# Moving the token-shift mixes and the convolution's SiLU products from VectorE to GpSimd in a Mamba block between two FFNs, with the steps placed anew

## What is computed

```python
def ffn(x, W_r, W_k, W_v, mu_r, mu_k):              # x has been normalised per token
    x_prev = shift x by one token, zeros first
    xr = mu_r * x + (1.0 - mu_r) * x_prev            # the token-shift mixes
    xk = mu_k * x + (1.0 - mu_k) * x_prev
    r = sigmoid(xr @ W_r.T)
    return r * (square(relu(xk @ W_k.T)) @ W_v.T)

def mamba(x, ...):
    xn = layernorm(x) * ln_w + ln_b
    xs, z = split(xn @ W_in.T)                       # 1024 channels each
    xc = silu(b_conv + causal convolution of xs with 4 taps)
    dt_low, B, C = split(xc @ W_xproj.T)             # 32, 16, 16
    delta = softplus(dt_low @ W_dt.T + b_dt)
    h = exp(delta * A) * h + delta * B * xc          # 1024 channels x 16 states, token by token
    y = (h * C).sum(states) + D_skip * xc
    return (y * silu(z)) @ W_out.T + x

x = x + 0.5 * ffn(layernorm(x), ...)
x = x + mamba(x, ...)
x = x + 0.5 * ffn(layernorm(x), ...)
```

## Time and profile before

| | us |
|---|---|
| median of 3 runs | 4891.49 |
| lowest and highest | 4890.23, 4892.57 |
| span of the profiled execution | 4888.0 |
| DVE busy | 4488.3 (92%) |
| PE busy | 4296.9 (88%) |
| POOL busy | 3196.4 (65%) |
| ACT busy | 2900.1 (59%) |

### The profile page before, as it was taken

One profiled execution on the slowest core, in us unless ns is written; L12 is line 12 of the kernel. 1 busy time (PEld: TensorE's weight loads), 2 busy tenths in 40 slices (PEclk: granted clock), 3 DMA queues, 4 the chain that ended last, 5 costly groups with the idle time before them and its releaser, 6 DMA issues.

```text
span 4888.0 us, 58099 instructions
## 1 busy us (share of the span) xinstructions
PE 4296.9 (88%) x16896; PEld 2382.9 (49%) x16896; DVE 4488.3 (92%) x3650; ACT 2900.1 (59%) x6355; POOL 3196.4 (65%) x3328
## 2 busy tenths in 40 slices
PE   6777989898999989989898899989999898999787
PEld 2444545454554545545454454545545454554443
DVE  2799999999999999999999999999999999999992
ACT  2555656666666566656666665666656666665452
POOL 1666767576676767767576676767667576776770
PEclk9888999999999999999999999999999999999798
DMA  2445555454554555555555554555555565655451
GB/s 82 141 135 180 172 171 185 163 183 162 189 169 151 189 168 186 172 173 185 158 174 163 186 172 152 190 179 176 172 185 173 155 180 156 190 170 153 167 164 62
DMA packets 423053, 810.71 MB, mean 166 GB/s; under 512 B 41264, under 2 KB 41264, under 8 KB 418640
## 3 DMA queue, kind: packets, MB, share of 16 engines
q1 hardware_dynamic: 422736, 807.00, 52.1%
HBM read 772.25 MB, written 34.60 MB: 165 GB/s over the span
## 4 chain that ended last, share of the span: by engine, by line
DVE 38%; PE 29%; issue 16%; ACT 7%; POOL 6%; DMA 3%; DVEq 0%; SPq 0%; POOLq 0%; ACTq 0%
DVE decay L1091 19%; DVE g L1099 10%; PE y_acc L567 6%; PE mm L494 5%; PE mm L483 5%; POOL dbx L1298 4%; PE mm L472 4%; DVE xc L1037 3%; DMA c_all<-bc_scratch 2%; PE mm L531 2%; PE mm L509 2%; PE mm L519 2%; DVE xc L1043 1%; ACT decay L889 1%; POOL xout L1287 1%
## 5 line engine op out<-in xcount | busy, mean ns | idle before, releaser
L1298 POOL TENSOR_TENSOR dbx<-u,b_all 128x1024 f32<-128x1024 f32 x1024 | 2414.2, 2358 | 902.6 <-DVE g L1099 901.7
L1091 DVE TENSOR_TENSOR_SCAN decay<-decay,state,dbx 128x1024 f32<-128x1024 f32 x1024 | 2405.4, 2349 | 172.4 <-ACT decay L889 157.6
L567 PE MATMUL y_acc<-ident,g 128*128 128x128 f32 x8192 | 1124.2, 283 | 372.5 <-DVE g L1099 370.6
L567 PEld LDWEIGHTS y_acc<-ident,g 128*128 128x128 f32 x8192 | 947.4, 144 | 939.1 <-DVE g L1099 713.2
L1099 DVE TENSOR_TENSOR g<-decay,c_all 128x1024 f32<-128x1024 f32 x1024 | 1244.3, 1215 | 10.0 <-DMA c_all<-bc_scratch 1.1
L886 ACT ACTIVATE decay<-delta,neg_a 128x512 f32<-128x512 f32 x1024 | 708.7, 692 | 36.9
L889 ACT ACTIVATE decay<-delta,neg_a 128x511 f32<-128x511 f32 x1024 | 686.9, 671 | 0.0
L895 ACT ACTIVATE state<-decay 128x2 f32<-128x2 f32 x1024 | 166.9, 163 | 508.6 <-DVE g L1099 506.1
L494 PE MATMUL mm<-wbuf_c,col 128*128 128x512 f32 x1024 | 460.9, 594 | 2.1 <-ACT col L758 1.3
L1037 DVE SCALAR_TENSOR_TENSOR xc<-mm,conv_sb,xc 128x509 f32<-128x509 f32 (+2 forms) x384 | 285.3, 743 | 47.0 <-ACT xs_last L804 35.7
L1302 POOL TENSOR_TENSOR dbx<-dbx,carry 128x1 f32<-128x1 f32 x1024 | 274.2, 268 | 80.3
(11 more groups left out here) (100 smaller groups left out, 5107.4 us busy)
## 6 DMA issues: line engine op xcount, KB each, us to landing
b_all<-bc_scratch SPq DMA_DIRECT2D x1024, 256.0 KB, 3.4
c_all<-bc_scratch SPq DMA_DIRECT2D x1024, 256.0 KB, 3.6
wbuf_d<-in_w_r SPq DMA_DIRECT2D x32, 1024.0 KB, 7.5
wbuf_c<-in_w_v SPq DMA_DIRECT2D x32, 1024.0 KB, 7.3
xin<-in_x SPq DMA_DIRECT2D x16, 1024.0 KB, 6.8
wbuf_c<-in_w_k SPq DMA_DIRECT2D x16, 1024.0 KB, 6.7
wbuf_d<-in_w_in SPq DMA_DIRECT2D x16, 1024.0 KB, 5.8
wbuf_a<-in_w_in SPq DMA_DIRECT2D x16, 1024.0 KB, 8.0
```

The source lines that it names most:

```text
L567: last = pe.matmul(y_acc[:, tb, j * P:(j + 1) * P], g[:, s % PAIRS, j, tb * P:(tb + 1) * P], ident[:, :], start=n == 0 and j == 0 and tb % ...
L1091: dve.tensor_tensor_scan(d, d, flat(dbx[:, s % DBX, :, :]), state[:, batch, s, 0:1], ALU.mult, ALU.add).then_inc(scan_done, 1)
L1298: pool.tensor_tensor(dbx[:, s % DBX, :, :], u[:, q % 2, :, :], b_all[:, s % BRING, :].unsqueeze(1).broadcast_to([P, QT, W]), ALU.mult).the ...
```

## The change

- The second half of every mix leaves DVE. ACT now also scales the current token, `mu * x`, in a pass of its own (`now`: into `rows` for one of the two mixes, in place in `col` for the other), and POOL adds the two (`ffn_mix_k`, `ffn_mix_r`): 256 instructions less on DVE, 256 more on ACT, 256 more on POOL.
- The SiLU product leaves DVE. ACT adds one to the tanh in place (with `unit`, a column of ones that it makes at the start by exp of zero), POOL multiplies: 128 less on DVE, 128 more on ACT, 128 more on POOL.
- In ffn1 the r mixes are now scaled ahead of the k mixes of the same step. `ffn_tanh` also waits for POOL's mix, since it overwrites `rows`; `xproj`, `make_u`, `skip_columns` and the first norm wait for POOL's product.
- Nearly all tables have new numbers; six of the eight zero products of an iteration go. `LOAD` (the steps at which SP issues weight and data loads) and `BANK` (which of two PSUM buffers a group of PE uses) are changed too.

The core of the diff:

```diff
-        SUM_SKIP = (5, 27, 35, 53)
-        OUT = ((4, 5), (19, 20), (21, 22), (23, 23))
-        MM_K = ((5, 7, 8, 9), (46, 47, 50, 51))
-        MM_R = ((10, 10, 12, 13), (41, 42, 44, 45))
+        SUM_SKIP = (1, 26, 35, 51)
+        OUT = ((4, 5), (18, 19), (21, 22), (23, 23))
+        MM_K = ((5, 7, 8, 9), (46, 48, 50, 51))
+        MM_R = ((10, 10, 11, 13), (41, 41, 44, 44))
...
-        XPROJ = (49, 50)
-        ZEROS = {2: 2, 31: 2, 39: 2, 30: 1, 53: 1}
+        XPROJ = (48, 50)
+        ZEROS = {31: 1, 33: 1}
...
-        BEFORE_K = ((3, 3, 5, 5), (39, 39, 40, 40))
-        BEFORE_R = ((6, 7, 7, 7), (37, 37, 38, 38))
-        RELU = ((7, 8, 9, 10), (49, 50, 53, 53))
-        TANH = ((11, 13, 14, 14), (42, 43, 45, 46))
+        BEFORE_K = ((3, 3, 4, 5), (40, 43, 43, 45))
+        BEFORE_R = ((3, 6, 6, 6), (36, 37, 38, 38))
+        RELU = ((7, 8, 11, 11), (49, 50, 51, 53))
+        TANH = ((12, 13, 14, 14), (42, 44, 45, 46))
...
-        XROWS = 51
-        MIX_K = ((3, 4, 5, 5), (42, 43, 45, 46))
-        MIX_R = ((6, 7, 7, 8), (38, 39, 40, 40))
-        CSILU = (33, 34, 40, 42, 43, 45, 48, 48)
+        XROWS = 52
+        MIX_K = ((4, 4, 6, 6), (43, 46, 46, 49))
+        MIX_R = ((4, 8, 8, 10), (39, 41, 41, 42))
+        CSILU = (36, 36, 43, 43, 45, 49, 51, 53)
...
+        def now(i, part, ct):
+
+            return rows[i][:, ct, :] if i == part else col[:, ct, 1:W + 1]
...
             def ffn_k(it, i, k, j):
-                pe.wait_ge(f_dve[i].sem, f_dve[i].at(k, "xk3"))
+                pe.wait_ge(f_pool[i].sem, f_pool[i].at(k, "xk3"))
...
                 act.activation(mix_k[:, ct, :], col[:, ct, 0:W], ACT.Copy,
                                scale=vec[:, 3, ct:ct + 1]).then_inc(f_act[i].sem, 1)
+                if i == 0:
+                    act.wait_ge(f_pe[0].sem, f_pe[0].at(k, "T3"))
+                else:
+                    act.wait_ge(f_act[1].sem, f_act[1].at(k, f"pk{ct}"))
+                act.activation(now(i, 0, ct), col[:, ct, 1:W + 1], ACT.Copy,
+                               scale=vec[:, 1, ct:ct + 1]).then_inc(f_act[i].sem, 1)
...
             def ffn_tanh(i, k, tb):
                 act.wait_ge(f_pe[i].sem, f_pe[i].at(k, f"r{tb}"))
+                act.wait_ge(f_pool[i].sem, f_pool[i].at(k, (f"xk{tb}", f"xr{tb}")[i]))
...
-                act.activation(rows[0][:, e % TB, :], xc2[:, e, :], ACT.Tanh, scale=0.5).then_inc(m_act.sem, 1)
+                    act.wait_ge(m_pool.sem, m_pool.at(k, f"silu{e - TB}"))
+                r = rows[0][:, e % TB, :]
+                act.activation(r, xc2[:, e, :], ACT.Tanh, scale=0.5).then_inc(m_act.sem, 1)
+                act.wait_ge(m_act.sem, m_act.at(k, f"th{e}"))
+                act.activation(r, r, ACT.Identity, bias=unit[:, 0:1]).then_inc(m_act.sem, 1)
...
-            def ffn_mix_k(i, k, ct):
-                dve.wait_ge(f_act[i].sem, f_act[i].at(k, f"pk{ct}"))
-                dve.scalar_tensor_tensor(out=mix_k[:, ct, :], in0=col[:, ct, 1:W + 1], scalar=vec[:, 1, ct:ct + 1],
-                                         in1=mix_k[:, ct, :], op0=ALU.mult, op1=ALU.add).then_inc(f_dve[i].sem, 1)
...
-            def conv_silu(k, e):
-                dve.wait_ge(m_act.sem, m_act.at(k, f"th{e}"))
-                o = xc2[:, e, :]
-                dve.scalar_tensor_tensor(out=o, in0=rows[0][:, e % TB, :], scalar=1.0, in1=o, op0=ALU.add,
-                                         op1=ALU.mult).then_inc(m_dve.sem, 1)
...
+            def conv_silu(k, e):
+                pool.wait_ge(m_act.sem, m_act.at(k, f"one{e}"))
+                o = xc2[:, e, :]
+                pool.tensor_tensor(o, o, rows[0][:, e % TB, :], ALU.mult).then_inc(m_pool.sem, 1)
...
+            def ffn_mix_k(i, k, ct):
+                pool.wait_ge(f_act[i].sem, f_act[i].at(k, f"ak{ct}"))
+                pool.tensor_tensor(mix_k[:, ct, :], mix_k[:, ct, :], now(i, 0, ct), ALU.add).then_inc(f_pool[i].sem, 1)
+
+            def ffn_mix_r(i, k, ct, mix_r):
+                pool.wait_ge(f_act[i].sem, f_act[i].at(k, f"ar{ct}"))
+                pool.tensor_tensor(mix_r[:, ct, :], mix_r[:, ct, :], now(i, 1, ct), ALU.add).then_inc(f_pool[i].sem, 1)
```

126 lines of the change are left out of this document (65 added, 61 removed), and 6 rows, old and new, of the table BANK.

## The result

The changed kernel takes 4828.97 us (median of 4 runs, 4820.82 to 4831.01) against 4892.03 for the kernel before on the same chip: a ratio of 0.987, 95% interval 0.985 to 0.988. It is faster, by 63 us and not by the 250 forecast, and lies outside the range.

A forecast was written before the change was run, and what follows sets the result against it. VectorE was taken to set the time, TensorE close behind. A chunk: 262.5 work + 7.5 + 3.9 + 0.6 waits = 274.5 us; the run: 4888.0 - 242 - 14 + 6 = 4638, stated as 4640, own range 4595 to 4700, overall 4500 to 4775.

The forecast's parts named there:

- The removal: VectorE, each chunk: 16 mixes and 8 SiLU products leave, 17.4 us less work, from 279.9 to 262.5.
- The price of 0.75 for a mix: VectorE: 0.75 us saved per mix, set above the 0.69 of scan pitch because mixes into `xn_col` last longer.
- GpSimd's lead: GpSimd stands three steps ahead, idling 56 us a chunk before its products; this covers 30.5 us of new adds.
- rival (c): GpSimd becomes the bound, each uncovered add delaying a scan by 1.27 us: slower, about 4910 us; chance 0.04.
- a pure saving, 5.2 us: TensorE, each chunk: six of eight zero matmuls go, taking its work from 264.6 to 259.4 us.
- Waits through ScalarE fall within these: Steps 4 to 23 and 40 to 59: ScalarE delays add nothing to VectorE's 7.5 and 3.9 us of waiting for TensorE.
- 0.6 us was kept for all the rest: Steps 24 to 39: small VectorE waits, 1.4 us before the change, were put at 0.6 us a chunk.
- 7.5 forecast: Steps 4 to 23: VectorE waits 7.5 us, from TensorE's 91.1 less VectorE's 77.2 and a carry of 6.45.
- the 6.45 carried out: After step 23: the two buffers of `g` let TensorE lag 6.45 us behind VectorE.
- 2 us late, and costs nothing of its own: Scan 5 comes 2 us late through ScalarE's extra pair at step 4, free because TensorE bounds the stretch it starts.
- (b): Waits through ScalarE add up at three places, 9 us a chunk more: about 4766 us; chance 0.18.
- (a): New step places fit the engines better; a chunk nears its longest engine, 266 us: about 4520 us; chance 0.13.

The follow-up runs named there:

- e4_pool_light: Changed kernel with GpSimd's 24 moved adds and products a chunk done on one column, not 512: 4821.7 us, 0.986 of the kernel before.
- e7_ops_alone: New instructions of all three engines with the old step tables, loads and zeros, one SiLU product moved from step 48 to 51: 4924.81 us, 1.006 of the kernel before.
- e15_zeros2: Changed kernel with the loads of before, two zero products put back at step 39 and two at step 2: 4738.74 us, 0.969 of the kernel before.
- e11_zeros39: Changed kernel with the loads of before and two removed zero products put back at step 39: 4739.05 us, 0.969 of the kernel before.
- e6_stats: Changed kernel with the loads of before and four statistics moved from steps 16, 17, 18, 18 to 18, 19, 20, 21: 4770.67 us.
- e10_k1_light: Changed kernel with the loads of before and two of four matmuls in each k group of the second FFN: 4714.23 us, 0.964 of the kernel before.
- e2_act_light: Changed kernel with ScalarE's 24 new passes a chunk done on one column, not 512: 4801.38 us, 0.981 of the kernel before.
- e14_all_light: Changed kernel, old loads, zeros at step 39, half of first FFN's k and r and second's k products, ScalarE's new passes on one column: 4567.64 us, 0.934.
- e1_load: Changed kernel with LOAD put back to the steps of before, except the B and C store and second z weights at 53: 4767.97 us, 0.975.
- e9_late_rows: Kernel before with the changed kernel's LOAD and nothing else: 4942.6 us, 1.010 of the kernel before.

## Why the prediction was wrong

**Right.** The removal: 17.4 us a chunk forecast, 17.0 measured (279.9 to 262.9). The price of 0.75 for a mix included the collision with GpSimd's one-element add, and that is gone: in the changed kernel its line reads, against the 523 of the earlier trace rows,

```profile
L1310 POOL TENSOR_TENSOR dbx<-dbx,carry x1024: 189/189/193, 154.3 to 4695.0; 128x1 f32<-128x1 f32 x171
```

so the trace after agrees with what was cited from the Trainium skill, "SBUF — State Buffer", "Who interferes with whom". TensorE 260.8 a chunk in place of 259.4, ScalarE 196.8 (197.6), GpSimd 222.4 (230; its carry adds lost 274.2 - 193.9 = 80 us in all, some 5 a chunk, with the collisions), the adds 1.18 to 1.27 us; GpSimd's lead covers them (`e4_pool_light`). Outside the 14 full chunks: 5.8 us more behind the last scan and 0.9 before the first (6 forecast); the first chunk gave 5.1 (9 forecast) and the last, from scan to scan, 1.6 (5 forecast), which is 7 us of the miss. The advice of the Trainium skill, "GPSIMD Engine Reference", "Engine selection", that elementwise work should stay on VectorE, cited in rival (c), does not hold here: GpSimd takes 1.18 to 1.27 us for an add where VectorE had some 0.75 for the whole second half of a mix, and yet these adds cost nothing by the chunk (`e4_pool_light`). With the new operations at the old steps it would have been right in its result: `e7_ops_alone` is 0.6% slower, with 121.3 us of VectorE's waits for GpSimd and 299.7 for ScalarE.

**Wrong, first: a term that was not in the sum.** The diff showed `LOAD`; the working never priced it. SyncE's queue is in order, the rows of C stand in it two steps ahead of their product, and a load that is put ahead of its release stops them. That is 3.6 us a chunk and 61 us by the medians.

**Wrong, second: the zeros.** They were taken off TensorE's work as a pure saving, 5.2 us. Two of them at step 39 filled a wait, and without them TensorE does the next group in part at 1.2 GHz: 1.9 us a chunk, 29 us over the run. The clock was thought of only at steps 0 to 3, where zeros at step 2 bring nothing that could be measured (`e15_zeros2`). With these two undone the chunk is 281.3, 6.8 over the forecast of 274.5.

**Wrong, third: the waits outside TensorE's account.** This is the largest part. The step that failed is that all waits of the two full stretches were put inside what TensorE's work, added up by stretch, left over ("Waits through ScalarE fall within these"), and that 0.6 us was kept for all the rest. In `e11_zeros39` VectorE is idle 18.8 us of a chunk, not 12.0: 9.5 in steps 4 to 23 (7.5 forecast), 5.5 in 40 to 59 (3.9), 3.7 in the other steps (0.6).

- In steps 4 to 23 the sum held as far as it went. The waits at 4 and 6 (3.4, decays) and at 12 to 14 (3.8) make 7.3, and TensorE has next to no pause from step 4 to 17 (at most 0.34 us in a step). It is busy 84.0 us in the stretch, as the working had it: 91.1 less the 6.45 carried out, 84.7. What came on top are 2.0 us at steps 16 and 18, 1.5 of them for GpSimd's add of the residual and 0.5 for a group of v. The sum has TensorE without a pause; behind these waits it idles 1.1 us at step 18 and 0.6 at 23, and the stretch is 86.3. `e6_stats` doesn't win this back by moving the statistics alone.
- In steps 40 to 59 the waits at 51 to 54, behind the groups of k, are 4.3 (`e10_k1_light` takes 3.3 of them away), and 0.65 us at step 45, for a decay, and small ones come on top.
- In the others, 2.1 us at 34 to 38 for decays, 0.4 at 32 for GpSimd, 0.3 at 1 and 0.3 at 61. TensorE has 9.8 us idle in steps 24 to 39, so its work is not what holds them, and no term of the sum stands for them. Those at 36 and 38 go when ScalarE's new passes are light (`e2_act_light`), that at 34 doesn't.

"2 us late, and costs nothing of its own" was said of scan 5. It comes 2.3 late in the changed kernel. By `e2_act_light` two thirds of what goes at 4 and 6 comes back at 8 and 12, so this was right for the greater part and not for the whole. That the sum comes near in the first stretch doesn't tell where VectorE will wait: the working had one delay at scan 15, and there are five waits up to it.

**The rivals.** The measured 4829 lies past (b), 4766. Its mechanism, waits that add up through ScalarE, was the likelier one: (b) put 9 us a chunk on the forecast's 274.5, and what is over it without the late rows is 6.8 + 1.9 = 8.7. That the two agree so well is luck: 1.9 of it is the clock at step 39, where (b) had the clock of steps 0 to 3 in mind, and some 2 are waits for GpSimd. The 3.6 for the late rows was in no case. (a) assumed that the new steps undo the waits; they do not.

**The sum of a chunk.** 274.5 + 6.8 (waits, third part) + 1.9 (clock) + 3.6 (late rows) = 286.8, which is what a chunk takes. 3.6 and 1.9 are differences of runs; 6.8 is what is left over, and by stretch it is 1.6 + 2.0 + 3.2.

**Open.** What the waits at step 4 to 6 come down to was taken apart only as far as ScalarE's new passes (1.78 of 2.28 stay with them at one column; `e14_all_light` has 1.76). The softplus with its two table loads stands there; it wasn't tried. The waits for GpSimd at 16 and 18 (0.7 and 0.8) stay in `e14_all_light` too; `e6_stats` took them away and got one of 1.3 at 19. For the decay at 34 (1.2) nothing was tried.

## What to carry to other kernels

When an engine is relieved, don't take the gain from stretch sums alone. They gave the waits well where TensorE works without a pause, and nothing elsewhere: follow each in-order queue (ScalarE, GpSimd, the engine that issues the DMAs) past every moved piece, and ask which release now comes last; a single wait priced at "hidden" needs the engine that hides it to be full at that place. A table of load steps is part of a schedule: an issue put ahead of its release holds back all loads behind it, and the ones with the least slack show it as "issue" time elsewhere. Work that looks like waste (products with zeros) may be holding TensorE's clock; before removing it, look at the granted clock at the spot, and put it back just there. Here the version with the loads of before and two zeros at step 39, 4739 us, beats both kernels.

## What the hardware showed that was not expected

- Two zero products of 512 columns in a wait of TensorE (1.88 us for 4 passes) made the following group take 3.60 us and not 4.81, and 29 us less in the run; with the zeros of before (2, 30, 31, 39 and 53, none at 33) the half clock came to step 35 and 29 us were lost again.
- GpSimd's add of 512 elements takes 1270 ns when its second operand is `rows` and 1180 when it is `col`, in both lines.
- A ScalarE pass of one column takes 0.28 to 0.30 us, one of 512 columns 0.71: making it small takes off only 0.42.
- The median landing time of the same 256 KB rows of C goes from 3.7 (`e1_load`) to 4.6 us (changed kernel), and from 3.6 (before) to 4.4 (`e9_late_rows`), by the steps at which other loads are issued; that of step 27, behind two transfers of 1 MB, from 3.7 to 9.3 in the mean.
